# Moving three projections between the stretches of a fused attention kernel, with a second buffer of normalised outputs

## The reference

```python
x = x + layernorm(attention(layernorm(x)))
x = x + layernorm(ffn(layernorm(x)))

def attention(x):                      # 16 heads of 64
    xn = layer_norm(x, ln_g, ln_b)
    q, k, v = xn @ wq + bq, xn @ wk + bk, xn @ wv + bv
    scores = q @ k.T / 8;  scores = where(key < query, -inf, scores)
    h = softmax(scores) @ v
    return h @ w0 + b0 + x

def ffn(x):                            # 8 experts of rank 16, two chosen
    gates = softmax of the two largest of x[:, 0] @ router_w.T
    return x + sum over experts of gate * (x @ down.T) @ up.T
```

## Time and profile before

| | |
|---|---|
| time, median of 3 | 996.57 us (996.43 to 998.4) |
| the profiled execution | 996.35 us, of which span 994.6 us |
| PE busy | 955.1 us (96%) |
| POOL busy | 701.7 us (71%) |
| DVE busy | 634.6 us (64%) |
| ACT busy | 536.1 us (54%) |
| granted clock of PE, mean | 0.995 |

### The profile page before, as it was taken

How to read it: one execution, slowest core, us unless ns; L and a number is a source line. 1 busy time by engine, 2 the same in 40 slices (tenths; PEclk the granted TensorE clock), 3 DMA queues, 4 the chain that set the end, 5 groups by cost and what they waited for, 6 DMA issues and landing times.

```text
span 994.6 us, 20388 instructions
## 1 busy us (share of the span) xinstructions
PE 955.1 (96%) x7662; PEld 600.4 (60%) x7662; DVE 634.6 (64%) x1869; ACT 536.1 (54%) x729; POOL 701.7 (71%) x517
## 2 busy tenths in 40 slices
PE   8899999999999999999999999999999999999995
PEld 3555656666666565666665666666666666666563
DVE  6666555555667657566757666756666665756377
ACT  5355546555455565765454565665455546555443
POOL 6378766667767767786676877776588676776752
PEclk9999999999999999999999999999999999999998
DMA  4001110011111000002100201110110200000110
GB/s 114 23 1 24 22 23 14 12 23 44 24 23 44 19 6 23 23 23 45 23 5 20 66 23 23 23 23 2 44 23 24 66 23 23 3 23 24 23 44 21
DMA packets 61837, 26.94 MB, mean 27 GB/s; under 512 B 39084, under 2 KB 53804, under 8 KB 61740
## 3 DMA queue, kind: packets, MB, share of 16 engines
q1 hardware_dynamic: 61708, 25.64, 11.0%
q10 hardware_dynamic: 32, 0.00, 0.0%
HBM read 22.76 MB, written 2.35 MB: 25 GB/s over the span
## 4 chain that ended last, share of the span: by engine, by line
PE 71%; POOL 14%; DVE 7%; ACT 4%; issue 3%; DMA 0%; POOLq 0%; ACTq 0%; DVEq 0%
PE po L770 20%; PE st L755 14%; POOL total L520 12%; PE st L680 9%; PE sc L718 7%; PE st L836 5%; PE st L750 5%; PE sc L780 3%; ACT ring L1048 3%; PE st L695 2%; DVE sc L1246 2%; PE st L696 1%; PE st L697 1%; POOL first_moments L477 1%; DVE least L1249 1%
## 5 line engine op out<-in xcount | busy, mean ns | idle before, releaser
L520 POOL TENSOR_TENSOR total<-total,ring 128x1024 f32<-128x1024 f32 (+1 forms) x313 | 539.0, 1722 | 246.2 <-PE po L770 204.7
L1246 DVE CUSTOM_DVE_ANT_0 sc<-sc,key_mask 128x512 f32<-128x512 f32 (+1 forms) x496 | 230.4, 522 | 142.2 <-PE sc L718 139.4
L1048 ACT ACTIVATE ring<-st 128x1024 f32<-128x1024 f32 (+1 forms) x256 | 228.5, 918 | 167.4 <-PE st L755 149.0
L1249 DVE TENSOR_REDUCE least<-sc 128x1 f32<-128x512 f32 x268 | 170.4, 678 | 74.9 <-PE sc L718 73.1
L770 PE MATMUL po<-ring,v_sb 128*64 128x512 f32 (+3 forms) x1280 | 210.7, 467 | 0.0
L755 PE MATMUL st<-q_high,k_low 64*128 64x512 f32 (+3 forms) x768 | 177.1, 447 | 0.0
L770 PEld LDWEIGHTS po<-ring,v_sb 128*64 128x64 f32 x1280 | 86.9, 137 | 129.5 <-issue 124.4
L718 PE MATMUL sc<-k_high,q_high 64*128 64x512 f32 (+3 forms) x768 | 135.5, 383 | 10.3 <-DVE least L1246 5.2
L755 PE MATMUL st<-q_high,k_high 64*128 64x512 f32 (+3 forms) x768 | 136.9, 343 | 0.0
L755 PE MATMUL st<-q_low,k_high 64*128 64x512 f32 (+3 forms) x768 | 136.8, 341 | 0.0
L718 PEld LDWEIGHTS sc<-k_high,q_high 64*128 64x128 f32 x768 | 69.0, 185 | 81.5 <-issue 64.4
(11 more groups left out here) (184 smaller groups left out, 1256.9 us busy)
## 6 DMA issues: line engine op xcount, KB each, us to landing
inv_row<-sums_dram SPq DMA_DIRECT2D x62, 256.0 KB, 3.9
x_a<-x SPq DMA_DIRECT2D x4, 512.0 KB, 5.1
sums<-sums_row SPq DMA_DIRECT2D x124, 2.0 KB, 2.1
x_b<-x SPq DMA_DIRECT2D x3, 512.0 KB, 5.7
out<-res_b SPq DMA_DIRECT2D x3, 512.0 KB, 4.7
total<-w_pairs SPq DMA_DIRECT2D x1, 1152.0 KB, 6.8
shift_row<-shift_t SPq DMA_DIRECT2D x62, 4.0 KB
x_a<-x SPq DMA_DIRECT2D x2, 256.0 KB, 3.0
```

The lines of the kernel that those rows point to most:

```text
L520: nc.gpsimd.tensor_tensor(so_far, so_far, tile_of(n, s)[:, :, col:col + w], ALU.add).then_inc(s_add, 1)
L1048: nc.scalar.activation(tile_of(n, s)[:, :, 0:w], st[s % 2][:, :, 0:w], ACT.Exp, scale=SCALE).then_inc(s_exp, 1)
L1246: last = nc.vector.tensor_tensor_reduce(bank[:, col:col + w], bank[:, col:col + w], key_mask[:, 0:w], -1.0, 3e38, ALU.add, ALU.min, least[ ...
L1249: last = nc.vector.tensor_reduce(least[:, h, a:a + 1], bank[:, col:col + w], AX.X, ALU.max, negate=True)
```

## The change

The keys of slot t + 2 move from stretch 1 to stretch 0 (bank 0), behind the queries. The outputs of slot t - 2 move from stretch 0 to stretch 2 (bank 1), behind the values; in slots with i of 1, 5 and 6 they go to stretch 1 (bank 0). The last slot keeps them in stretch 0 (bank 1). `u` and `mix`, which were in bank 0 of stretch 1, are now in bank 1. `o_norm` has two buffers, so `normalise(n)` waits for the `out` fill of n - 2. The statistics of norm 2 (places 4 and 5) move one place later, and POOL's root of norm 2 moves from stretch 0 to stretch 1 of the slot with i of 2.

```diff
-        if t + 2 < N:
-            found.append(((("q", t + 2, 0), ("k", t + 2, 0), ("v", (t + 2) // 2, t % 2))[g], x))
+        if g == 0 and t + 2 < N:
+            found += [(("q", t + 2, 0), x), (("k", t + 2, 0), y)]
+        if g == 2 and t + 2 < N:
+            found.append((("v", (t + 2) // 2, t % 2), x))
+        if g == (1 if i in (1, 5, 6) else 2) and 2 <= t < N - 1:
+            found.append((("out", t - 2, 0), y))
         if g == 0:
-            if 2 <= t < N:
-                found.append((("out", t - 2, 0), y))
+            if t == N - 1:
+                found.append((("out", t - 2, 0), x))
...
         if after and (i, g) == (5, 1):
-            found.append((("u", c - 1, 0), y))
+            found.append((("u", c - 1, 0), x))
...
         if after and (i, g) == (6, 1):
-            found.append((("mix", c - 1, 0), y))
+            found.append((("mix", c - 1, 0), x))
...
-    ROOT_TIMES = [(1, 1, 0, 1), (2, 0, 2, 0), (4, 1, 3, 0), (7, 2, 4, 0)]
+    ROOT_TIMES = [(1, 1, 0, 1), (2, 1, 2, 0), (4, 1, 3, 0), (7, 2, 4, 0)]
...
-        o_norm = sb("o_norm", [P, S])
+        o_norm = [sb(f"o_norm{i}", [P, S]) for i in range(2)]
...
             def normalise(n):
...
-                if n:
-                    wait_filled(pool, "out", n - 1, 0)
-                nc.gpsimd.tensor_tensor(o_norm[:], o_raw[n % 2][:], inv_row[:], ALU.mult).then_inc(s_norm, 1)
+                if n > 1:
+                    wait_filled(pool, "out", n - 2, 0)
+                nc.gpsimd.tensor_tensor(o_norm[n % 2][:], o_raw[n % 2][:], inv_row[:], ALU.mult).then_inc(s_norm, 1)
...
             def after_scores(b, place):
 
-                if place == 4:
+                if place == 5:
                     wait_taken(dve, "out", PAIRS * (b + 1) - 1, 0)
                     norm_stats(2, acc[b % 2], low)
-                elif place == 5:
+                elif place == 6:
                     norm_stats(2, acc[b % 2], high).then_inc(s_var, 1)
```

## The result

The changed kernel takes 1003.81 us (median of 4 runs, 1003.41 to 1005.52), the kernel before 996.50 on the same chip (996.41 to 998.4): a ratio of 1.0071, 95% interval 1.006 to 1.0083. It is slower, by some 7 us. The prediction was 998.5, with a range up to 1002.5. The profiled execution took 1003.60 us; its span is 1001.9, where that of before was 994.6.

A forecast was written before the change was run, and what follows sets the result against it. PE was taken to bound the kernel (28.11 of 28.44 us in a plain slot). Terms of -2.5, -1.6, -0.8, +1.4, -0.2, +6.4, -0.8 made +1.9 us on the profiled 996.35, so 998.25, median 998.5, range 994 to 1002.5.

The forecast's parts named there:

- A plain slot, -0.19: Thirteen ordinary slots: -0.40 in stretch 0, -1.58 in stretch 1, +1.79 in stretch 2, so -0.19 us each, -2.5 together.
- The boundary between S step and `weigh`: Stretch 1, with the keys gone: `weigh` right behind the S step costs no more than before, charged 0.
- rival D: Boundaries cheaper: 0.16 us less at each `weigh` behind an S step, -2.9, and 1.8 more; about 994 us; chance 0.15.
- The eight slots, +0.80: Slots 5, 6, 13, 14, 21, 22, 25, 29: outputs wait 0.90 us for step 6's exponentials; +0.80 each, +6.4 together.
- Rival C: Stretch 1 of the eight slots: step 6's exponentials are in time, no wait is paid; 991 us; chance 0.1.
- Slots 9, 17, 11, 19, 27, 24: POOL's wait hides the losses of later stretches, stretch 0's saving remains: -0.40 us each, -0.8 and -1.6 together.
- Slot 16, -0.8: DVE held to the end of `res_b`, then taking the outputs in 1.22 us: 534.0 against 534.8, -0.8 us.
- Keys' cover: Stretch 0, keys taken directly behind queries: costed at nothing, with 0.6 us of cover before DVE's first maximum.
- Rival A: Every slot: `k_low` ends late, stretch 1's second S step waits; 8.7 us per 0.3 beyond; 1007 us; chance 0.05.
- Slot 30 itself waited already, and had no q and k: 0.: Slot 30, stretch 1: it already waited for ACT's exponential and projects no queries or keys, so charged 0.
- Slot 1 ... its saving in stretch 1 turns into a longer wait for POOL: Slot 1: no outputs yet, six more products in stretch 0, +1.4 us; stretch 1's saving becomes waiting for POOL.
- Rival B: POOL holds DVE's small norm 2 statistics around slots 9, 17, 25 and in 16: 1003 us, or 1001; chance 0.15.

The follow-up runs named there:

- Experiment 5: The changed kernel with keys, outputs, `u` and `mix` of slots 5, 6, 13, 14, 21, 22, 25, 29 in their old places: 998.31 us.
- Experiment 1: The changed kernel with the outputs of slot 30 alone put back into stretch 0: 998.46 us, ratio to the kernel before 1.0009.
- Experiment 4: The changed kernel with nine unread products of zeros ahead of the sum fill of slot 30: 1000.84 us, ratio to the kernel before 1.0029.
- Experiment 3: The changed kernel with the keys of slot 1 alone put back into stretch 1: 1000.74 us, ratio to the kernel before 1.0033.
- experiment 2: The changed kernel with twelve unread products of zeros ahead of the sum fill of slot 2: 1002.75 us, ratio to the kernel before 1.0054.
- Experiment 7: The changed kernel with the keys of slot 1 in stretch 1 and the outputs of slot 30 in stretch 0: 995.59 us, ratio 0.9983.
- Experiment 8: The changed kernel with unread products of zeros, twelve ahead of slot 2's sum fill and nine for slot 30's: 999.34 us, ratio 1.002.
- experiment 6: The changed kernel with old places in slots 5, 6, 13, 14, 21, 22, 25, 29, slot 1's keys and slot 30's outputs put back: 988.58 us.

## Why the prediction was wrong

The steps of the sum held, but for two.

- *A plain slot, -0.19.* Measured -0.20 to -0.29, mostly -0.25. In slot 3 the twelve products of queries and keys take 2.99 us to `weigh` (134.31 to 137.30), and the outputs behind `v` 1.88 (153.25 to 155.13), as in the sum. The boundary between S step and `weigh`, which I charged at 0, holds; rival D, with 0.16 less at each, did not come. The remaining 0.06 a slot is some 0.8 us over the thirteen plain slots; its place isn't shown.
- *The eight slots, +0.80.* Measured +0.83 to +0.89. The wait of 0.90 read in slot 30 was there in all of them. Rival C falls. Experiment 5 isolates this term: 6.9 us for eight slots, where the sum had 6.4.
- *Slots 9, 17, 11, 19, 27, 24.* -0.39 to -0.47, for -0.40. POOL's wait hid what I said it would.
- *Slot 16, -0.8.* -1.11. DVE was held twice again, the second time to the end of `res_b`, as I worked out:

```profile
532.07 1.46 DVE L1227 TENSOR_SCALAR first_moments<-first_moments 128x4 f32<-128x4 f32 x1
...
533.51 2.33 DVE L1230 TENSOR_SCALAR first_moments<-first_moments 128x4 f32<-128x4 f32 x1
535.76 1.21 DVE L1316 TENSOR_TENSOR acc<-st,acc 128x1024 f32<-128x1024 f32 x1
```

The second ends at 535.84, with POOL's `res_b`, which began at 533.45 and took 2.37. PE's gap fell from the 1.78 us of the earlier trace rows to 0.88.

- *Keys' cover.* `k_low` was in time: no slot has a longer wait at the second S step of stretch 1. Rival A falls.
- ***"Slot 30 itself waited already, and had no q and k: 0."*** This is the step that failed, by 4.6 us. I looked at what the slot gets in stretch 1 and not at what it loses in stretch 0. In every other slot the keys take the place of the outputs ahead of `weigh`; in slot 30 nothing does, so `weigh` and POOL's chain come 2 us sooner against DVE, POOL's additions hold two of DVE's gate operations, and PE waits 3.08 us for the maxima behind them. Experiments 1 and 4 show it: either the outputs or useless products in that place bring DVE's operations from 2.1 and 2.3 us to 0.17.
- ***"Slot 1 ... its saving in stretch 1 turns into a longer wait for POOL", +1.4.*** The wait came, to 0.01 us. But it was charged at its length alone, and the clock was at 1.2 GHz behind it: 1.5 us more in slot 2, for which the sum had nothing. Experiment 3 gives both back.
- *Rival B* named the right mechanism at the wrong place. It came to 1003 by DVE's statistics in slots 9, 17, 25 and 16. For norm 2, the first of the two operations was held once in slots 9 and 17 (1.68 us instead of 0.17) and the second slipped through, as my sum had it; in slot 25 neither was held. These slots pay next to nothing: the last S step of slots 9 and 17, with what lies ahead of the sum, takes 0.42 and 0.40 us, for 0.35 in a plain slot. Slot 16, which it put at a loss of 2.0, gained 1.11. The held operations that cost time are the gate's, in slot 30. That the time landed near the rival's is chance.

Each of the two long operations of slot 30 ends within 0.03 us of an addition of POOL. By the Trainium skill (SBUF — State Buffer, "Who interferes with whom") a `tensor_scalar` can take the pair of ports shared with GpSimd, and a DVE operation with two inputs in SBUF contends with a GpSimd operation that reads SBUF. The trace agrees. L1283, with two inputs in SBUF too, took 0.17 us: it began at 923.01, between POOL's additions (one ended at 922.95, the next began at 923.12).

So the change is a gain of 0.25 in a plain slot, 0.4 where POOL is late, and 1.1 in slot 16; the eight slots spend 7.0 us of it, the two gaps 8.2 with their clock. What is not settled: why the same gap brings the lower clock in some executions and not in others. The gap of slot 1 had full clock behind it in the profiles of experiments 1 and 4, that of slot 30 in experiment 2's; in the profiles after, of experiment 3 and of experiment 5 every such gap had the lower clock behind it. The kernel before also has two groups of runs, near 996.8 and near 998.3 (ten of 27 in the last comparison), though its longest gap between the first sum and the last slot is the 1.78 us of slot 16, which the change shortens to 0.88. Experiments 7 and 8 have no second group. Whether it comes from that gap no run tests, and from what length a gap costs clock stays open.

## What to carry to other kernels

When a fill moves away from a place, list the slots in which nothing takes its place (the first and the last ones of a pipeline above all) and lay all engines' operations of these slots beside each other again: the engine that comes earlier may now meet short operations of another that it had missed by a microsecond. Leaving ten of 32 slots in the old order was worth 15 us here, twice what the change had lost. And price a new gap on TensorE above its length where it comes near 3 us: here by 1.5 to 1.6 us more behind four of the five such gaps that the profiles show with the lower clock, and by 2.85 behind the fifth.

## What the runs showed of the hardware

- Behind a gap of 2.9 to 3.1 us on PE the granted clock was 0.50 to 0.52 (1.2 GHz) for some 3.4 us of work in the profile after, and 0.61 in the mean over 8.5 us in experiment 5. In other executions the same gaps left it at 1.00 (experiments 1 and 4 behind slot 1's, experiment 2 behind slot 30's). Behind the gap of 1.28 us in slot 1 of experiment 6 the products kept their spacing of 0.23.
- The granted clock was 0.50 for 3.4 us in the last slot of the kernel before, behind 1.9 us of products of one column and 1.1 of products of 128, with no idle time above 0.2 us ahead of them.
- An addition of 128x1024 on POOL can stretch a DVE operation on 8 columns from 0.17 to 2.29 us, thirteen times as long; the operation between the two long ones took 0.17, and it began in the gap of 0.17 us between two additions.
- 1.8 us of useless products on PE made the kernel 3 us faster (1003.81 to 1000.84), because they kept two other engines apart.
